# A cross-attention and quantized FFN kernel: every engine's calls up to tile 6 are issued in another order

## The reference, cut to what matters

```python
def reference(x, ctx_1024, g_xattn, g_ffn, Wk, Wv, bv, Wq, bq, Wo, bo, w_gate, w_up, w_down):
    # x (8, 512, 512), ctx (8, 77, 512); w_gate, w_up (1408, 512), w_down (512, 1408)
    kp = ctx @ Wk.T; vp = ctx @ Wv.T + bv; qp = layernorm(x) @ Wq.T + bq
    attn = softmax(qp @ kp.T / sqrt(512)) @ vp @ Wo.T + bo
    x = x + tanh(g_xattn) * attn
    # fp4: blocks of 16 along the last axis, scale = max|.|/6, values rounded to the E2M1 grid
    def fp4_linear(a, w): return fp4(a) @ fp4(w).T
    h = silu(fp4_linear(layernorm(x), w_gate)) * fp4_linear(layernorm(x), w_up)
    return x + tanh(g_ffn) * fp4_linear(h, w_down)
```

## Time and profile before

| | us |
|---|---|
| median of 3 runs (lowest, highest) | 833.4 (832.52, 834.1) |
| span of the profiled execution | 832.3 |
| PE busy in it | 822.4 |
| DVE busy | 650.7 |
| ACT busy | 459.9 |
| POOL busy | 400.5 |

### The profile page before, as it was taken

One profiled execution on the slowest core, in us unless ns is written; L12 is line 12 of the kernel. 1 busy time (PEld: TensorE's weight loads), 2 busy tenths in 40 slices (PEclk: granted clock), 3 DMA queues, 4 the chain that ended last, 5 costly groups with the idle time before them and its releaser, 6 DMA issues.

```text
span 832.3 us, 11653 instructions
## 1 busy us (share of the span) xinstructions
PE 822.4 (99%) x4102; PEld 417.0 (50%) x4102; DVE 650.7 (78%) x967; ACT 459.9 (55%) x930; POOL 400.5 (48%) x333
## 2 busy tenths in 40 slices
PE   9999999999999999999999999999999999999998
PEld 5555445444554445444544454445544454444445
DVE  5887899898998698877878688778876878776654
ACT  2778675547555666456563755366646565344320
POOL 3498797764334353444333543454444533444421
PEclk9999999999999999999999999999999999999999
DMA  9723703553243434532641255224433443222232
GB/s 318 285 70 103 157 13 97 122 128 92 48 80 106 108 82 89 129 56 54 114 120 40 55 110 136 61 60 99 97 61 61 85 85 73 58 54 55 48 75 73
DMA packets 192817, 78.21 MB, mean 94 GB/s; under 512 B 176387, under 2 KB 178037, under 8 KB 192759
## 3 DMA queue, kind: packets, MB, share of 16 engines
q1 hardware_dynamic: 192759, 77.47, 39.6%
HBM read 22.76 MB, written 8.39 MB: 37 GB/s over the span
## 4 chain that ended last, share of the span: by engine, by line
PE 93%; ACT 3%; DVE 2%; issue 1%; DMA 1%; POOL 1%; POOLq 0%; ACTq 0%; DVEq 0%
PE banks L1918 60%; PE banks L2037 27%; DVE banks L1417 1%; PE banks L2053 1%; PE banks L1912 1%; PE banks L1971 1%; PE banks L1999 1%; PE banks L1998 1%; PE banks L2143 1%; DMA x_T<-x_parts 1%; PE banks L2150 0%; PE banks L2008 0%; PE banks L2160 0%; PE banks L2165 0%; PE banks L2155 0%
## 5 line engine op out<-in xcount | busy, mean ns | idle before, releaser
L1918 PE MATMUL banks<-wgu_hi,x_T 128*128 128x512 f16 (+1 forms) x1536 | 439.3, 361 | 1.6 <-DMA x_T<-x_parts 0.9
L1918 PE MATMUL banks<-wgu_lo,x_T 128*128 128x512 f16 (+1 forms) x768 | 277.5, 361 | 0.0
L1918 PEld LDWEIGHTS banks<-wgu_hi,x_T 128*128 128x128 f16 x1536 | 150.3, 98 | 155.6 <-issue 1.3
L2037 PE MATMUL banks<-wd,arena 128*128 128x512 f16 x1023 | 227.2, 379 | 0.0
L2037 PEld LDWEIGHTS banks<-wd,arena 128*128 128x128 f16 x1023 | 99.7, 98 | 117.4 <-issue 0.6
L648 POOL TENSOR_TENSOR arena<-arena,h_r 128x1024 f32<-128x1024 f32 (+1 forms) x60 | 93.2, 1554 | 115.3 <-DVE h_r L1372 115.3
L648 POOL TENSOR_TENSOR arena<-arena,h_s 128x1024 f32<-128x1024 f32 x64 | 90.7, 1418 | 88.6 <-DVE arena L1419 53.6
L1918 PEld LDWEIGHTS banks<-wgu_lo,x_T 128*128 128x128 f16 x768 | 75.1, 98 | 76.8 <-issue 0.3
L648 POOL TENSOR_TENSOR xwork<-xwork,x_s 128x512 f32<-128x512 f32 x32 | 38.4, 1201 | 152.0 <-DVE xwork L1419 152.0
L1052 ACT ACTIVATE arena<-banks,scal 128x512 f32<-128x512 f32 (+1 forms) x96 | 61.9, 647 | 84.9 <-PE banks L1918 84.8
L1571 DVE SCALAR_TENSOR_TENSOR arena<-arena,scal,banks 128x512 f32<-128x512 f32 (+1 forms) x90 | 62.2, 694 | 56.3 <-PE banks L1918 53.5
(11 more groups left out here) (199 smaller groups left out, 1043.6 us busy)
## 6 DMA issues: line engine op xcount, KB each, us to landing
ring<-in_x_dram SPq DMA_DIRECT2D x8, 1024.0 KB, 5.1
out_dram<-ring SPq DMA_DIRECT2D x31, 256.0 KB, 2.2
arena<-in_L_ffn_w_down_dram SPq DMA_DIRECT2D x4, 704.0 KB, 5.0
arena<-in_L_ffn_w_gate_dram SPq DMA_DIRECT2D x5, 512.0 KB, 9.7
arena<-in_L_ffn_w_up_dram SPq DMA_DIRECT2D x5, 512.0 KB, 9.6
ring<-in_L_xattn_Wk_dram SPq DMA_DIRECT2D x4, 256.0 KB, 6.1
ring<-in_L_xattn_Wq_dram SPq DMA_DIRECT2D x4, 256.0 KB, 6.8
wd<-in_ctx_dram SPq DMA_DIRECT2D x1, 1024.0 KB
```

The lines of the kernel that those rows point to most:

```text
L1918: ended = e.matmul(at, l, r, start=(i == 0), stop=(i == len(terms) - 1))
L2037: ended = e.matmul(by_k(down_ps(t)[:, :], KD), l, r, start=(k == 0 and i == 0), stop=(k == KH - 1 and i == 2))
```

## The change

Calls change places within the hand-written part, on all five engines; no call, buffer, wait or size is added or removed, and the loop from tile 7 on is the same. The diff is cut to the places that the prediction speaks of.

```diff
@@ -593,9 +593,9 @@
...
     move_values(5)
+    move_down(1)
     move_values(6)
     move_values(7)
-    move_down(1)
     move_down(2)
...
@@ -1153,32 +1153,32 @@
...
     ln1_stats(0)
     wo_copy(0)
     wo_copy(1)
     key_copy(2)
-    key_copy(3)
     wo_copy(2)
     wo_copy(3)
+    key_copy(3)
+    key_copy(4)
     gu_folds(0, EARLY)
+    ln1_apply(0)
     vo_copy(0)
-    key_copy(4)
-    ln1_apply(0)
-    gu_squares(5)
     gu_high(0)
     gu_high(1)
+    gu_squares(5)
     gu_low(0)
+    gu_squares(6)
+    gu_low(1)
     xn_copy(0, 0)
-    gu_low(1)
-    gu_squares(6)
     gu_high(2)
     gu_high(3)
...
@@ -1187,49 +1187,49 @@
...
+    xn_copy(0, 2)
+    gu_squares(7)
     vo_copy(2)
     gu_folds(5, NPAIR)
-    gu_squares(7)
+    gu_low(4)
     gu_squares(8)
-    gu_low(4)
     gu_low(5)
-    xn_copy(0, 2)
     gu_high(6)
     gu_high(7)
     gu_low(6)
     gu_low(7)
-    gu_high(8)
-    gu_high_of(6)
     gu_squares(9)
     vo_copy(3)
+    gu_high_of(6)
+    gu_high(8)
     xn_copy(0, 3)
-    ln1_stats(1)
     gu_high(9)
     gu_high_of(7)
+    gu_low(8)
     gu_high_of(8)
-    gu_low(8)
+    ln1_stats(1)
     exps(0)
     prob_copy(0)
-    gu_low(9)
     gu_squares(10)
     gu_high_of(9)
     gu_high(10)
     key_copy(5)
     x_stats(0)
+    gu_low(9)
     key_copy(6)
     x_apply(0)
+    key_copy(7)
     x_stats(1)
-    key_copy(7)
     gu_high_of(10)
     x_squares(0)
     key_copy(8)
...
@@ -1237,35 +1237,35 @@
...
     x_high(1)
+    down_folds()
     down_squares(2)
-    down_folds()
     ln1_apply(1)
...
@@ -1687,20 +1687,20 @@
     gu_scales(2)
     gu_tops(3)
     gu_round(0)
+    gu_scales(3)
+    gu_tops(4)
     gu_round(1)
-    gu_tops(4)
-    gu_scales(3)
-    gu_scales(4)
...
@@ -1715,18 +1715,18 @@
...
     down_tops(0)
     gu_round(8)
-    gu_round(9)
     value_row()
     softmax(0)
+    gu_round(9)
+    down_tops(1)
     sums(0)
     value_rows(0)
     values(0, 0)
     gu_round(10)
     values(0, 1)
-    down_tops(1)
     x_scales(0)
+    x_divide(0)
     values(0, 2)
-    x_divide(0)
     x_round(0)
...
@@ -1734,19 +1734,19 @@
...
     values(0, 3)
-    x_scales(1)
+    power_of('d', pow_d)
     value_rows(1)
-    power_of('d', pow_d)
+    down_scales(2)
     x_divide(1)
-    down_scales(2)
+    down_power()
+    x_round(1)
+    value_rows(2)
     down_scales(3)
-    x_round(1)
-    down_power()
-    value_rows(2)
+    down_round(0)
     value_rows(3)
     value_rows(4)
-    down_round(0)
     down_round(1)
...
@@ -1799,19 +1799,19 @@
...
     finish(1)
     h_low(2, 0)
-    h_low(2, 1)
     h_round(3, 0)
     x_scales(5)
-    h_scales(3, 1)
+    h_low(2, 1)
+    x_divide(5)
     hidden(4, 0)
-    x_divide(5)
     x_round(5)
     value_tops()
     hidden(4, 1)
+    x_low(5)
     hidden(4, 2)
-    x_low(5)
     h_round(3, 1)
...
@@ -2196,10 +2196,10 @@
     vo_product(0)
     gu_turn(0)
     gu_turn(1)
+    att_turn(0, 0)
     vo_product(1)
     gu_subtract(0)
     gu_subtract(1)
-    att_turn(0, 0)
     vo_product(2)
...
@@ -2225,18 +2225,18 @@
...
     gu_subtract(8)
+    key_product(5)
     att_scores(0, 3)
-    key_product(5)
+    value_product(0)
     key_product(6)
-    value_product(0)
     prob_turn(0)
     gu_turn(10)
     gu_subtract(9)
     att_values(0, 0)
     att_values(0, 1)
     att_values(0, 2)
+    key_product(7)
     gu_subtract(10)
-    key_product(7)
     att_values(0, 3)
     gu_turn(11)
...
@@ -2245,10 +2245,10 @@
...
     value_product(3)
-    value_product(4)
     power_spread('d', pow_d)
     gu_subtract(11)
     gate_up(0, 0, 0)
+    value_product(4)
     gate_up(0, 1, 0)
...
@@ -2296,26 +2296,26 @@
...
     gate_up(4, 2, 0)
+    att_turn(2, 0)
     gate_up(4, 2, 1)
+    att_turn(2, 1)
     down(2, 0)
-    att_turn(2, 0)
-    att_turn(2, 1)
+    att_scores(2, 0)
     down(2, 1)
+    gate_up(5, 0, 0)
+    att_scores(2, 1)
     att_turn(2, 2)
-    att_scores(2, 0)
-    att_scores(2, 1)
+    down(2, 2)
     top_turn('v', top_v[0:KEYS, :])
-    down(2, 2)
-    gate_up(5, 0, 0)
     gate_up(5, 0, 1)
+    gate_up(5, 1, 0)
...
```

More of the change, by code:

```diff
@@ L759, in pool_program @@
             gu_times(10)
+            x_stats(1)
             ln1(1)
-            x_stats(1)
             x_times(0)
@@ L1155, in scalar_program @@
             gu_squares(3)
+            w.wait_ge(loads['gates'], 32)
+            e.activation(tanh_a, tanh_a, ACT.Tanh).then_inc(tanh_done, 1)
+            gu_squares(4)
             w.wait_ge(bqk_turned, 1)
             e.copy(bqk_col[:, :], bank[turn_bank['bqk', 0]][:, 0:KD]).then_inc(bqk_sb, 1)
-            w.wait_ge(loads['gates'], 32)
-            e.activation(tanh_a, tanh_a, ACT.Tanh).then_inc(tanh_done, 1)
             e.activation(tanh_f, tanh_f, ACT.Tanh).then_inc(tanh_done, 1)
-            gu_squares(4)
             key_copy(0)
@@ L1225, in scalar_program @@
             key_copy(8)
+            gu_high(11)
             x_high(0)
@@ L1228, in scalar_program @@
             x_apply(1)
-            gu_high(11)
             x_stats(2)
+            gu_low(10)
             x_squares(1)
-            gu_low(10)
             gu_low(11)
@@ L1256, in scalar_program @@
             down_high_of(2)
-            gate_silu(1, 1)
             exps(1)
@@ L1263, in scalar_program @@
             gate_silu(2, 0)
+            prob_copy(1)
             h_squares(0, 1)
-            gate_silu(2, 1)
-            prob_copy(1)
             x_high(3)
             h_high(0, 0)
+            gate_silu(2, 1)
             h_high(0, 1)
@@ L1284, in scalar_program @@
             x_high(4)
+            x_apply(5)
             h_high(2, 0)
             h_high(2, 1)
-            x_apply(5)
+            h_squares(3, 0)
             gate_silu(4, 0)
-            h_squares(3, 0)
             ln1_stats(2)
@@ L1303, in scalar_program @@
             x_apply(6)
+            xn_copy(2, 2)
             x_stats(7)
             h_squares(4, 1)
-            xn_copy(2, 2)
             gate_silu(5, 0)
+            x_squares(6)
             xn_copy(2, 3)
-            x_squares(6)
             x_high(6)
@@ L1699, in vector_program @@
             gu_tops(10)
-            scale_bo()
             gu_top_of()
@@ L1703, in vector_program @@
             gu_scales(6)
+            scale_bo()
             power_of('gu', pow_gu)
@@ L1758, in vector_program @@
             down_round(2)
+            hidden(0, 2)
             x_low(2)
-            hidden(0, 2)
             x_scales(3)
@@ L1764, in vector_program @@
             softmax(1)
+            x_divide(3)
+            sums(1)
             hidden(1, 1)
             h_scales(0, 1)
-            x_divide(3)
-            sums(1)
             x_round(3)
@@ L1822, in vector_program @@
             h_low(3, 0)
+            power_of('v', pow_v, KEYS)
             h_low(3, 1)
-            power_of('v', pow_v, KEYS)
             x_round(6)
             key_tops()
+            finish(2)
             hidden(5, 0)
-            finish(2)
             hidden(5, 1)
+            softmax(2)
             h_scales(5, 0)
-            softmax(2)
+            x_scales(7)
+            x_low(6)
             value_power()
-            x_low(6)
-            x_scales(7)
+            power_of('k', pow_k)
+            value_low(2)
             hidden(5, 2)
-            power_of('k', pow_k)
             h_low(4, 0)
-            value_low(2)
             prob_low(2)
+            x_divide(7)
             h_low(4, 1)
-            x_divide(7)
             h_scales(5, 1)
@@ L2212, in tensor_program @@
             att_scores(0, 0)
+            att_scores(0, 1)
             gu_subtract(4)
-            att_scores(0, 1)
             gu_subtract(5)
@@ L2260, in tensor_program @@
             gate_up(1, 0, 0)
+            att_scores(1, 1)
             gate_up(1, 0, 1)
-            att_scores(1, 1)
             gate_up(1, 1, 0)
@@ L2275, in tensor_program @@
             gate_up(2, 1, 1)
+            att_values(1, 0)
             gate_up(2, 2, 0)
[L2277 removed]
             att_values(1, 1)
+            gate_up(2, 2, 1)
             att_values(1, 2)
[L2280 removed]
             gate_up(3, 0, 0)
@@ L2284, in tensor_program @@
             gate_up(3, 1, 1)
+            att_values(1, 3)
             gate_up(3, 2, 0)
+            down(0, 0)
             gate_up(3, 2, 1)
-            down(0, 0)
             down(0, 1)
-            att_values(1, 3)
             down(0, 2)
@@ L2316, in tensor_program @@
             att_scores(2, 2)
+            att_scores(2, 3)
             top_turn('k', top_k)
-            att_scores(2, 3)
             down(3, 0)
@@ L2328, in tensor_program @@
             gate_up(6, 2, 0)
+            down(4, 0)
+            att_values(2, 0)
+            att_values(2, 1)
             gate_up(6, 2, 1)
-            att_values(2, 0)
-            down(4, 0)
-            att_values(2, 1)
             down(4, 1)
```

41 lines of the change are left out of this document (21 added, 20 removed).

## The result

The changed kernel takes 837.41 us (median of 4 runs, 837.26 to 838.14) where the kernel before takes 833.22 (4 runs, 832.52 to 834.1): a ratio of 1.0053, 95% interval 1.0040 to 1.0065. It is slower by 4.2 us; the forecast was 831.5 us, and its range ended at 835.0. The profiled execution has a span of 836.4 us against 832.3.

A forecast was written before the change was run, and what follows sets the result against it. PE's own work was taken to bound the kernel from tile 1 on; an earlier DVE chain to x_low(1) starts it 1.9 us sooner, giving an 830.4 us span, 831.5 us with the 1.1 us offset; range 829.4 to 835.0 us.

The forecast's parts named there:

- The bound: From tile 1 on the kernel lasts as long as PE's own work; order only shifts its start, 127.06 us, or adds holes.
- The fold: 41 to 52 us: POOL's first result 1.7 us late, yet 0.6 us gained net at vo_product(2), bounds 0 and 1.4.
- ACT's order: 52 to 80 us: calls spread between copies put exps(0) at 77.9 instead of 79.57 us; bounds 0.5 and 2.2 us.
- DVE's hole: At the softmax: filling DVE's 4.50 us idle brings x_round(0) to 90.4 from 93.35 us, 2.9 us gained, bounds 1 and 3.5.
- DVE to `x_low(1)`: From x_round(0): 24.7 us of work, 0.4 for a load, two POOL meetings; x_low(1) ends at 120.6 against 122.44 us.
- Two meetings: POOL's down_divide(3) at down_round(0) and first down_times at down_round(1) each cost DVE 2.57 us before x_low(1).
- the second case: Rival, 12%: one DVE meeting with POOL is spared, x_low(1) ends 2.57 us sooner, PE's floor almost binds: 829.1 us.
- only changes places: PE before tile 1: value_product(4) behind gate_up(0, 0, 0) costs nothing; DVE's last value row comes after down_round(0).
- The 1.9 us: Gain at tile 1: 1.8 us from x_low(1) ending earlier plus 0.1 for the shorter way of hidden(0, 0).
- Behind 127 us: Tile 1 on: forward PE calls are ready, closest gate_up(5, 0, 0); booked 0, bound 1.3 us for a late transpose.
- `att_turn(2, i)`: Moved PE calls behind 127 us, booked at 0 together with down(0, 0), down(4, 0) and the SP order.
- The slower one: Rival, 15%: POOL bounds before 95 us, its 1.7 us delay reaches x_round(0), x_low(1) ends 2.9 us late: 836.3 us.

The follow-up runs named there:

- e3: Kernel before with the early part alone (moves up to DVE's down_round(0) and their neighbours on the other engines): 832.05 us, ratio 0.9989.
- e5: Changed kernel with one place taken back, on DVE x_low(2) ahead of hidden(0, 2) again: 834.78 us, ratio 1.0019.
- e6: Kernel before with one swap alone, on DVE hidden(0, 2) ahead of x_low(2): 835.89 us, ratio 1.0031.
- e9: Changed kernel with x_low(2) ahead of hidden(0, 2) again and PE's order of before for tiles 4 to 6: 833.40 us, ratio 1.0002.
- e10: Kernel before with hidden(0, 2) ahead of x_low(2), and x_divide(3), sums(1) ahead of hidden(1, 1), on DVE: 838.06 us, ratio 1.0062.
- e4: Kernel before with all of the change except the early moves up to DVE's down_round(0) and neighbours: 838.79 us, ratio 1.0064.
- e1: Changed kernel with DVE's x_divide(3) and sums(1) behind hidden(1, 1) and h_scales(0, 1) again: 838.15 us, ratio 1.0068.

## Why the prediction was wrong, point by point

- **The bound** was read rightly up to a point: PE is saturated from tile 1 on. "An order can only shift the moment at which PE enters this saturated stretch ... or put a new hole into it" is what happened, and the hole was the larger of the two.
- **The fold.** Direction right, size short: `vo_product(2)` at 50.30 instead of 51.52 us, a gain of 1.2, near the upper bound of 1.4, where 0.6 was taken. The step that was off is DVE's `gu_round(3)` ahead of POOL: POOL came first, at 43.08, so PE's `gu_turn(0)` did not wait.
- **ACT's order.** `exps(0)` at 78.47; forecast 77.9 with 0.5 to 2.2 us gained, measured 1.1.
- **DVE's hole.** Filled, as said. `x_round(0)` at 91.77 instead of the 90.4 forecast: the term was sized 2.9 us and measured 1.6, within its bounds. `gu_round(9)` met POOL again (2.32 us for its first pass), but this is not what set the time: behind it DVE waited 2.12 us for ACT's `x_apply(0)`, which waited 1.19 us for POOL's `x_stats(0)`. POOL came to that at 86.21 us, behind its pair of `gu_low_of` (5.43 us from 80.69), 1.4 us earlier than before. So the earlier start of `x_stats(0)` was sized too large, and POOL was what held it.
- **DVE to `x_low(1)`.** Two meetings at 2.57 us were booked, one happened (3.89 instead of 1.62 us for one pass), the second was spared, the second case's mechanism by another pair: while `down_round(1)` ran, POOL's small `x_stats(3)` instructions took 1.90 and 1.93 us (the same lines took 0.19 and 0.54 for `x_stats(0)`), so POOL's `down_times(0)` began at 119.42, when `x_low(1)` had just ended. `x_low(1)` ended at 119.41, forecast 120.6; tile 1 started at 124.32, forecast 125.2. The errors of this and the step before cancelled in part, which is luck. PE did not wait for `x_T`, though 2 to 3 us were forecast: its lead at `value_product(1)` was 1.9 us and not 2.6, and it then waited 1.01 us at `att_turn(1, 0)` for ACT's `ln1_apply(1)` (0.28 before), so it asked for tile 1 4.9 us behind the issue of the transpose. That `value_product(4)` "only changes places" held in this trace; in those of e3 and e5 PE waited 0.6 and 0.7 us at `power_spread('d')`, which it no longer covers.
- **The baseline.** The 1.9 us were counted from a profiled execution in which a late transpose had cost 0.93 us, and the offset of 1.1 us to the median hid that; the offset of one execution's time to its own span is 1.8 us. By the medians the early part gives 0.8 us (e3).
- **Behind 127 us: the step that failed.** "Every PE call that moved forward must be ready. ... I book 0". Only PE's own moves were gone through, and what feeds one of them; `gate_up(5, 0, 0)`, named as the closest, never waited. The diff's DVE hunks at tiles 1 to 3, `hidden(0, 2)` and `x_low(2)` above all, were not costed, though the part on `x_low(1)` had just shown what such a meeting costs. In its place the runs showed 2.9 us for that swap alone (e6) and 2.6 us within the change (e5). The hole in the changed kernel was 4.43 us long, and the lower clock behind it cost 1.65 us, which the prediction did not have at all ("no part of this is a matter of PE's speed"). `att_turn(2, i)`, booked at 0, costs too once the hole is gone: PE's late order is worth 1.4 us (e5 against e9). In the trace of after PE does not wait there. Some 1.1 us of the late moves stay open.
- **The rivals.** The slower one (POOL late by 1.7 us before 95 us, 836.3 us) came near the time by another mechanism; its own did not occur, since POOL started 0.8 us earlier than the forecast had it. POOL did set `x_round(0)`, as this rival said, but earlier than before and not later.

The Trainium skill, page "SBUF — State Buffer", section "Who interferes with whom", which the prediction weighed, is borne out: `hidden`, with one input in PSUM, is never held up (its 96 instructions in the trace of after take 0.60 to 0.75 us), and `x_low`, with both in SBUF, is (0.68 or 2.77 us), by whoever starts first. Its rule also names DVE instructions in a two-port mode, which the prediction left out; the `x_scales` TENSOR_SCALAR with its one input in SBUF (L1540), 0.18 us with POOL idle and up to 2.17 us under a POOL instruction in the trace of after, fits that; no run shows in which mode it ran.

## What to carry to other kernels

When a change gives a saturated engine a lead, go through the deadlines of every engine that feeds it, not only through its own moved calls: here each microsecond of lead was met by the next due (`hidden(0, 2)`, `hidden(1, 1)`, `gate_silu(1, 2)`, `ln1_apply(2)`). Where two engines hold each other up for whole instructions, look at who is released by whom. Here the instruction directly behind the one that releases the other engine began 0.16 us ahead of it; so the one that can be held up belongs there, and one that can't goes behind it. And take the baseline from more than one execution's span before an effect of a microsecond is booked as gain.

## What the runs showed of the hardware that was not expected

- Two DVE instructions of 0.60 and 0.68 us, swapped, differ by 2.1 us in sum: `x_low(2)` took 0.68 us where it began 0.15 or 0.16 us ahead of POOL and 2.77 where it began 0.37 behind (the same in every trace of either order). POOL's instruction is the longer one when it comes second, 2.97 against 2.59 us.
- Holes of 2.2 us (e10) and 2.6 us (e1) left PE's granted clock at 1.00; after holes of 3.3 us (e4) and 4.4 us (after) it stood at 0.50 for some 3 us, which added about 1.6 us.
- The transpose that fills `x_T` was there within 3.5 us in one execution of the same kernel and took 4.6 in another, enough to move the whole span by 0.9 us. PE asks for tile 1 3.5 to 3.7 us behind its issue in the kernel before, and 4.9 us behind it in the changed one, which did not wait.
